# A bidirectional Mamba layer with a ternary FFN gate: larger h1 fetches and bias adds on VectorE in the last stage

## The reference

```python
xn  = layernorm(x)                                # x: 8 x 2048 x 1024
fwd = mamba(xn, weights_f)                        # D_INNER 2048, 16 states, conv of 4
bwd = flip(mamba(flip(xn), weights_b))
s   = concat([fwd, bwd], -1) @ wproj.T + bproj    # 2048 -> 1024
Wq1, Wq2 = ternary(W1), ternary(W2)               # round(W / mean|W|) clipped to -1..1
h1  = relu(xn @ Wq1.T + b1)                       # 1024 -> 4096
g   = silu(h1 @ Wq2.T + b2)                       # 4096 -> 1024
out = x + s * g
```

## Time and profile before

| | |
|---|---|
| Median of 3 runs | 6874.6 us (6847.4 to 6888.3) |
| Profiled execution, its own time | 6843.6 us |
| Its span, slowest core (core 6) | 6841.7 us; cores 6816.6 to 6841.7 us |
| Busy share: TensorE, VectorE, ScalarE, GpSimd | 43%, 68%, 31%, 8% |
| Mean granted clock of TensorE | 0.677 on core 6, 0.679 to 0.682 on the others |
| DMA | 302.29 MB, mean 44 GB/s |
| Last stage | from about 6012 us to the end, some 830 us |

### The profile page before, as it was taken

The page is one execution under the profiler, slowest core; times in us unless marked ns, Lnnn a source line. Parts: engine busy times, 40 slices in busy tenths (PEclk is TensorE's granted clock), DMA queues, the critical chain, the costliest instruction groups (busy, mean ns, idle before and its releaser), DMA issues. The chain is left out here.

```text
span 6841.7 us, 36862 instructions; the slowest of 8 cores (6816.6 to 6841.7 us)
## 1 busy us (share of the span) xinstructions
PE 2958.1 (43%) x8194; PEld 944.2 (14%) x8194; DVE 4660.7 (68%) x5288; ACT 2118.8 (31%) x3486; POOL 538.4 (8%) x974
## 2 busy tenths in 40 slices
PE   2053334333433334333444454444444433456776
PEld 1010001110110011101111111111111111112222
DVE  3228886888778876888688858885888589700000
ACT  3023333333333333333333333334333433300000
POOL 0100000000000000000100000000000000012221
PEclk9965556655665656555766676667666756668888
DMA  6521111111111111111311111111111100031111
GB/s 196 137 42 46 24 23 46 23 23 26 45 25 22 23 32 38 23 27 24 77 33 34 32 55 31 33 36 50 36 31 33 49 22 22 23 94 59 57 58 57
DMA packets 152694, 302.29 MB, mean 44 GB/s; under 512 B 56464, under 2 KB 73504, under 8 KB 149408
## 3 DMA queue, kind: packets, MB, share of 16 engines
q0 software_dynamic: 88784, 240.77, 15.0%
q1 hardware_dynamic: 63696, 59.18, 2.8%
HBM read 330.31 MB, written 50.59 MB: 56 GB/s over the span
## 5 line engine op out<-in xcount | busy, mean ns | idle before, releaser
L733 ACT ACTIVATE dA_sl<-delta_sb,A_sb 128x512 bf16<-128x512 bf16 x2048 | 1309.2, 710 | 2512.1 <-DVE h_sl L785 2094.7
L800 PE MATMUL py<-h_sl,ident 128*128 128x512 bf16 x2048 | 911.6, 596 | 2626.4 <-DVE h_sl L785 2068.3
L759 DVE TENSOR_TENSOR_SCAN h_sl<-dA_sl,hcar,dBu_sb 128x512 bf16<-128x512 bf16 x1024 | 1231.3, 1264 | 27.7 <-DVE dBu_sb L748 1.4
L766 DVE TENSOR_TENSOR_SCAN h_sl<-dA_sl,hcar,dBu_sb 128x512 bf16<-128x512 bf16 x1024 | 1231.3, 1263 | 27.3 <-DVE dBu_sb L748 0.9
L748 DVE TENSOR_TENSOR dBu_sb<-du_sb,B_bc 128x2048 bf16<-128x2048 bf16 x512 | 624.8, 1220 | 324.8 <-ACT dA_sl L733 284.4
L800 PEld LDWEIGHTS py<-h_sl,ident 128*128 128x128 bf16 x2048 | 231.1, 127 | 3251.7 <-issue 3236.9
L536 PE MATMUL pdb<-xn_cm,wslot 128*128 128x512 bf16 x1024 | 436.2, 603 | 557.1 <-DMA wslot<-win_sl_f 272.1
L785 DVE TENSOR_TENSOR h_sl<-h_sl,C_bc 128x2048 bf16<-128x2048 bf16 x512 | 627.3, 1225 | 56.0 <-DVE hcar L776 4.5
L1093 DVE TENSOR_TENSOR sstage<-px,g_sb 128x512 bf16<-128x512 f32 x16 | 11.0, 687 | 729.4 <-PE px L1078 729.4
L447 PE MATMUL pw<-xn_cm,w1f 128*128 128x512 bf16 x1024 | 402.1, 563 | 0.0
L536 PE MATMUL px<-xn_cm,wslot 128*128 128x512 bf16 x1024 | 326.5, 477 | 46.0 <-DMA wslot<-win_sl_f 46.0
(11 more groups left out here) (130 smaller groups left out, 2789.1 us busy)
## 6 DMA issues: line engine op xcount, KB each, us to landing
wslot<-win_sl_f POOLq DMA_DIRECT2D x128, 256.0 KB, 4.2
wslot<-win_sl_b POOLq DMA_DIRECT2D x128, 256.0 KB, 3.9
xst<-x SPq DMA_DIRECT2D x32, 512.0 KB, 4.3
wstg<-w1t_sl POOLq DMA_DIRECT2D x8, 2048.0 KB, 9.4
wstg<-w2t_sl POOLq DMA_DIRECT2D x32, 512.0 KB, 4.1
B_bc<-bc_scr POOLq DMA_DIRECT2D x8, 2048.0 KB, 8.0
C_bc<-bc_scr POOLq DMA_DIRECT2D x8, 2048.0 KB, 12.7
qst<-w1t_sl POOLq DMA_DIRECT2D x64, 256.0 KB, 3.8
```

The lines of the kernel that those rows point to most:

```text
L733: e.activation(out=o, in_=i, func=AF.Exp, scale=sc),
L759: e.tensor_tensor_scan(out=o, data0=d0, data1=d1, initial=i, op0=ALU.mult, op1=ALU.add),
L766: e.tensor_tensor_scan(out=o[:, ::-1], data0=d0[:, ::-1], data1=d1[:, ::-1], initial=i, op0=ALU.mult, op1=ALU.add),
L800: e.matmul(out=o, lhsT=ident[:], rhs=r, start=st, stop=sp), sPE if last else None)
```

## The change

The h1 fetch takes four slices at a time: one DMA brings 4 x 128 x 256 tokens (256 KB) into a buffer of four times the size, and 16 matmuls follow it. The bias matmuls are gone: the first matmul of each bank opens the accumulation itself, the two bias rows are loaded broadcast over 128 partitions, and VectorE adds them. In the passes it adds b2 from PSUM into a bf16 staging tile, which ScalarE's SiLU then reads in place of PSUM. In the projection it adds bproj from PSUM into `sstage`, and multiplies by g in a second instruction. TensorE's wait for the projection weights ahead of the first pass is gone too (the one ahead of the projection stays), and VectorE has one for the bias rows.

```diff
-            b.dma("gpsimd", sBulkG, b2r_sb[:], dr["b2row"])
-            b.dma("gpsimd", sBulkG, bpr_sb[:], dr["bprojrow"])
+            b.dma("gpsimd", sBulkG, b2bc[:],
+                  dr["b2row"].unsqueeze(1).broadcast_to([1, P, D]))
+            b.dma("gpsimd", sBulkG, bpbc[:],
+                  dr["bprojrow"].unsqueeze(1).broadcast_to([1, P, D]))
...
-                    if c == 0 and ps == 0:
-                        b.wait("tensor", sV, v_on)
-                        b.wait("tensor", sBulkG, v_wp)
-                    for i4, (tt, hf) in enumerate(tiles):
-                        b.op("tensor", lambda e, o=banks[i4][:],
-                             w=ones34[0:1, 0:P],
-                             r=b2r_sb[0:1, hf * TC:(hf + 1) * TC]:
-                             e.matmul(out=o, lhsT=w, rhs=r, start=True, stop=False))
-                    for ft in range(NFT):
-                        par = ft % 2
+                    for g4 in range(NG4):
+                        par = g4 % 2
...
                         vh = b.dma("gpsimd", sems[par],
-                                   h1sl[:, (ps * 2 + par) * HB:
-                                        (ps * 2 + par + 1) * HB],
-                                   h1_scr[ft][:, t0 + ps * 2 * P:
-                                              t0 + ps * 2 * P + 2 * P])
+                                   h1sl[:, (ps * 2 + par) * 4 * HB:
+                                        (ps * 2 + par + 1) * 4 * HB],
+                                   h1_scr[4 * g4:4 * (g4 + 1),
+                                          :, t0 + ps * 2 * P:t0 + ps * 2 * P + 2 * P]
+                                   .transpose([1, 0, 2]))
...
+                        for sub in range(4):
+                            ft = 4 * g4 + sub
...
-                    b.wait("scalar", sPE, v)
+                    b.wait("vector", sPE, v)
+                    if c == 0 and ps == 0:
+                        b.wait("vector", sBulkG, v_wp)
                     for i4, (tt, hf) in enumerate(tiles):
+                        gsl = gstage[:, hf * TC:(hf + 1) * TC]
...
+                        vv = b.op("vector", lambda e, o=gsl, pb=banks[i4],
+                                  bb=b2bc[:, hf * TC:(hf + 1) * TC]:
+                                  e.tensor_add(out=o, in0=pb[:], in1=bb), sV)
+                        b.wait("scalar", sV, vv)
...
-                            pb=banks[i4]:
-                            e.activation(out=o, in_=pb[:], func=AF.Silu), sA)
+                            i=gsl:
+                            e.activation(out=o, in_=i, func=AF.Silu), sA)
...
-                        b.op("tensor", lambda e, o=bank[:], w=ones34[0:1, 0:P],
-                             r=bpr_sb[0:1, hf * TC:(hf + 1) * TC]:
-                             e.matmul(out=o, lhsT=w, rhs=r, start=True, stop=False))
...
-                        v_m = b.op("vector", lambda e, o=ssl, pb=bank,
+                        v_a = b.op("vector", lambda e, o=ssl, pb=bank,
+                                   bb=bpbc[:, hf * TC:(hf + 1) * TC]:
+                                   e.tensor_add(out=o, in0=pb[:], in1=bb), sV)
+                        b.wait("vector", sV, v_a)
+                        v_m = b.op("vector", lambda e, o=ssl, a1=ssl,
                                    a2=g_sb[:, tl * D + hf * TC:
                                            tl * D + (hf + 1) * TC]:
-                                   e.tensor_mul(out=o, in0=pb[:], in1=a2), sV)
+                                   e.tensor_mul(out=o, in0=a1, in1=a2), sV)
```

More of the change, by code:

```diff
@@ L948, in build_program @@
         with ExitStack() as p34:
-            ones34 = p34.enter_context(nc.sbuf_tensor("ones34", [1, P], F32))
-            b2r_sb = p34.enter_context(nc.sbuf_tensor("b2r_sb", [1, D], F32))
-            bpr_sb = p34.enter_context(nc.sbuf_tensor("bpr_sb", [1, D], F32))
+            b2bc = p34.enter_context(nc.sbuf_tensor("b2bc", [P, D], F32))
+            bpbc = p34.enter_context(nc.sbuf_tensor("bpbc", [P, D], F32))
+            gstage = p34.enter_context(nc.sbuf_tensor("gstage", [P, 2 * TC], BF16))
             w2q_sb = p34.enter_context(nc.sbuf_tensor("w2q_sb", [P, NFT * D], BF16))
-            h1sl = p34.enter_context(nc.sbuf_tensor("h1sl", [P, 2 * TC], BF16))
+            h1sl = p34.enter_context(nc.sbuf_tensor("h1sl", [P, 8 * TC], BF16))
             g_sb = p34.enter_context(nc.sbuf_tensor("g_sb", [P, 4 * D], BF16))
@@ L958, in build_program @@
             sstage = p34.enter_context(nc.sbuf_tensor("sstage", [P, 2 * TC], BF16))
-            v_on = b.op("vector", lambda e: e.memset(ones34[:], 1.0), sV)
-            b.dma("gpsimd", sBulkG, b2r_sb[:], dr["b2row"])
-            b.dma("gpsimd", sBulkG, bpr_sb[:], dr["bprojrow"])
+            b.dma("gpsimd", sBulkG, b2bc[:],
+                  dr["b2row"].unsqueeze(1).broadcast_to([1, P, D]))
+            b.dma("gpsimd", sBulkG, bpbc[:],
+                  dr["bprojrow"].unsqueeze(1).broadcast_to([1, P, D]))
             for jj in range(NKD):
@@ L985, in build_program @@
                        [(2, 0), (2, 1), (3, 0), (3, 1)], sH1G2)]
+            NG4 = NFT // 4
             for c in range(NCH):
@@ L997, in build_program @@
                             b.wait("tensor", sV, pj_out[4 * (c - 1) + 3])
-                    if c == 0 and ps == 0:
-                        b.wait("tensor", sV, v_on)
-                        b.wait("tensor", sBulkG, v_wp)
-                    for i4, (tt, hf) in enumerate(tiles):
-                        b.op("tensor", lambda e, o=banks[i4][:],
-                             w=ones34[0:1, 0:P],
-                             r=b2r_sb[0:1, hf * TC:(hf + 1) * TC]:
-                             e.matmul(out=o, lhsT=w, rhs=r, start=True, stop=False))
-                    for ft in range(NFT):
-                        par = ft % 2
-                        prev = h1mm.get((c, ps, ft - 2)) or \
-                               (h1mm.get((c - 1, ps, NFT - 2 + ft))
-                                if ft < 2 and c > 0 else None)
+                    for g4 in range(NG4):
+                        par = g4 % 2
+                        prev = h1mm.get((c, ps, g4 - 2)) or \
+                               (h1mm.get((c - 1, ps, NG4 - 2 + g4))
+                                if g4 < 2 and c > 0 else None)
                         if prev:
@@ L1034, in build_program @@
-                        h1mm[(c, ps, ft)] = v
-                    b.wait("scalar", sPE, v)
-                    for i4, (tt, hf) in enumerate(tiles):
+                            b.wait("tensor", sW2s[g4 // (NG4 // 2)],
+                                   w2half[g4 // (NG4 // 2)])
+                        for sub in range(4):
+                            ft = 4 * g4 + sub
+                            for i4, (tt, hf) in enumerate(tiles):
+                                last = (i4 == 3 and sub == 3)
+                                v = b.op("tensor", lambda e, o=banks[i4][:],
+                                         w=h1sl[:, (ps * 2 + par) * 4 * HB
+                                                + sub * HB + (tt - 2 * ps) * P:
+                                                (ps * 2 + par) * 4 * HB
+                                                + sub * HB + (tt - 2 * ps + 1) * P],
+                                         r=w2q_sb[:, ft * D + hf * TC:
+                                                  ft * D + (hf + 1) * TC],
+                                         st=(ft == 0), sp=(ft == NFT - 1):
+                                         e.matmul(out=o, lhsT=w, rhs=r, start=st,
+                                                  stop=sp), sPE if last else None)
@@ new lines, in build_program @@
+                        h1mm[(c, ps, g4)] = v
+                    b.wait("vector", sPE, v)
+                    if c == 0 and ps == 0:
+                        b.wait("vector", sBulkG, v_wp)
+                    for i4, (tt, hf) in enumerate(tiles):
+                        gsl = gstage[:, hf * TC:(hf + 1) * TC]
+                        ps_prev = gsil.get((c, tt - 1, hf)) if i4 >= 2 else \
+                            (gsil.get((c - 1, 3, hf)) if ps == 0 and c > 0 else
+                             gsil.get((c, 1, hf)) if ps == 1 else None)
+                        if ps_prev:
+                            b.wait("vector", sA, ps_prev)
+                        vv = b.op("vector", lambda e, o=gsl, pb=banks[i4],
+                                  bb=b2bc[:, hf * TC:(hf + 1) * TC]:
+                                  e.tensor_add(out=o, in0=pb[:], in1=bb), sV)
+                        b.wait("scalar", sV, vv)
@@ L1076, in build_program @@
                                                 k * D + (hf + 1) * TC],
-                                     st=False, sp=last:
+                                     st=(k == 0), sp=last:
                                      e.matmul(out=o, lhsT=w, rhs=r, start=st,
```

## The result

The changed kernel takes 6491.1 us, median of 8 runs (6480.6 to 6514.0), against 6865.7 for the kernel before (8 runs, 6847.4 to 6888.3): the ratio is 0.9456, 95% interval 0.9438 to 0.9474. That is 375 us less, where 371 had been forecast. The profiled execution took 6505.6 us, its slowest core, again core 6, a span of 6504.0.

What follows compares the result with a forecast made beforehand. Last-stage passes were taken to lose time to h1 fetch waits through two buffers and to slow matmuls. 6064 + 2 + 4 × 99.4 + 7.2 gave 6471 us, forecast as 6504 against the median; range 6450 to 6590.

Steps and rivals of the forecast that it cites:

- The loop through the h1 buffer: In the passes, refilling a buffer sets the cadence: 3.85 us per two fetches before, 7.54 with four-tile fetches landing in 3.3.
- rival (c): h1 fetch: landing grows with the bytes, to 8.8 us, so batching keeps the wait; +132 us, 6636; chance 0.05.
- (b): h1 fetch: slower than its bytes suggest, landing in 6.2 us; +70 us, 6574; chance 0.1.
- (e): h1 fetch: queued behind wproj and catsl, lands in 25.7 us, kernel slower than before; +538 us, 7040; chance 0.02.
- The pass: Last stage: a pass over h1 falls from about 72 us to 29.5 us at full clock.
- a pass stalls only before groups 2, 4 and 6: In a pass: groups 0 and 1 are prefetched at no cost, leaving three stalls of 0.63 us on top of 27.6.
- The bias part: Passes and projection: f32 bias matmuls leave TensorE, eight took 7.1 us at half clock; VectorE adds instead, 0.69 us each.
- The projection: After each chunk's passes: the chain of VectorE output, store, catsl and matmuls takes 40.4 us in place of 48.7.
- The start: Start of the last stage: dropping the wproj wait gains little; first h1 matmul at 6064 us, as before (6064.14).
- The sum: Core 6, whole kernel: start, four chunks of 99.4 us and the end give 6471 us, 371 less than before.
- rival (a): Passes and projection: dense matmuls don't keep the full clock, granted clock stays at 0.76; +72 us, 6576; chance 0.2.
- the half clock inside today's passes goes with its sparse cadence: In the passes: denser matmuls, busy 3.45 of 3.77 us, get full clock, above 0.95, in place of 0.66 to 0.76.

Runs made afterwards that it cites:

- the ring of four: The changed kernel with its four 256 KB h1 buffers used as one ring over both passes: 6459.5 us, ratio 0.9420 to before.
- the four buffers: The changed kernel with its h1 buffers as one ring, plus four buffers in place of two for catsl and the x tile: 6423.5 us, ratio 0.9370.
- the reordered start: The changed kernel with its h1 buffers as one ring, plus bias rows and wproj loaded behind the first h1 fetches: 6427.1 us, ratio 0.9381.
- The last kernel: Changed kernel with h1 ring, four catsl and x buffers and late loads, plus a wait for each eighth of W2 instead of each half: 6392.9 us, ratio 0.9314.
- all three edits: The changed kernel with h1 buffers as one ring, four catsl and x buffers, and bias rows and wproj loaded late: 6402.3 us, ratio 0.9337.

## Why the prediction was right, point by point

**The loop through the h1 buffer** was the right cause, and its terms too. The landing was taken at 3.3 us and is 3.4, the period of two groups at 7.54 and is 7.54 to 7.60. The runs separate it from its rivals: more buffers in rotation with the old fetch give most of the gain (274 of 314 us), so the size of the DMA as such isn't it; a fetch of twice the size doesn't land twice as late (2.6 against 2.2 us), so rival (c) fell; and rivals (b) and (e) fell with the landing of 3.4.

**The pass** was mis-sized a little: 31.2 us at full clock (two passes from the end of the last matmul of chunk 3's projection, 6395.06, to 6457.45) in place of 29.5. The step "a pass stalls only before groups 2, 4 and 6", by 0.63 each, is what failed. The stalls listed are 1.58, 0.54 and 0.23 in this pass 0. By the starts of its matmuls TensorE stands still for 3.4 us in it, before groups 2, 4, 5, 6 and 7, and for 3.8 us in the pass 1 behind it, before groups 2, 3, 5 and 7, where 1.9 had been forecast: the 1.7 us more per pass are these. One reason is the landing, which isn't always 3.4: the fetch before the stall of 1.58 took 4.4 us, and one in pass 1 took 4.7. What delayed them was not looked into. With the ring of four the stalls are gone, and 25 us with them.

**The bias part** alone was expected to bring about 70 us and brought 70, and the passes kept their waits. VectorE's adds do lie beside the matmuls in the passes, and where they don't, their price was right: the output of a tile takes 4.02 us (forecast 4.0), the end of the stage 6504.0 − 6496.79 = 7.2 (7.2), and the first projection matmul starts 1.79 us after the pass (2.0), released by SiLU behind the add.

**The projection** takes 6496.79 − 6457.45 = 39.3 us at full clock, forecast 40.4. Its chain is the one that the prediction followed, and its price is shown by the four buffers: 34 us of the kernel's time, and a projection without a gap.

**The start** gains nothing, as forecast: 6066.93 against 6064, and 64.5 against 64.9 us from the end of the second block's work. The broadcasts land 8.9 and 12.6 us after their issue, the second above the 10 us of the upper bound. That the order of the loads at the start is the cause is shown by the reordered start, with 27 us; how much of it is the fetch's place in GpSimd's queue, and how much the quicker load of W2, no run separates.

**The sum.** From the first h1 matmul to the last one of the projection core 5 needs 6452.43 + 7.07 − 6048.05 = 411.5 us, where 400 had been forecast; these are core 5's first and last rows:

```profile
6048.05 0.59 PE L1029 MATMUL pdb<-w2q_sb,h1sl 128*128 128x512 bf16 x1 [56.50 <-DMA h1sl<-h_scr]
...
6452.43 7.07 PE L1084 MATMUL pd<-wproj_sb,catsl 128*128 128x512 bf16 x32 [0.73 <-DMA catsl<-cat_scr]
```

The 12 us more are mainly the 1.7 us per pass. Core 6, the slowest, needed 6496.79 − 6066.93 = 429.9. That is rival (a) in small: the clock of cores 6 and 7 was lower for a while. The profiled execution was therefore 33 us above the sum for it (6505.6 against 6473): 12 from the passes, 18 from the clock and 3 from the later start.

That the median comes out within 13 us of the forecast is in part luck. The sum was 12 us too low, and the 31 us by which the median of three runs lay above the profiled execution of the kernel before were added to it. Nothing ties these 31 us to the changed kernel, whose profiled execution lay 14 above its median. With eight runs of before the same median is 9 us lower (6865.7).

**The clock.** The step "the half clock inside today's passes goes with its sparse cadence" held: 1.00 in the pass at 6395 us, and in the one at 6177 us 0.81, which is not the half clock but rival (a). What it was worth is an estimate from the rows, as no run holds the clock and takes away the waits alone. Today's cadence of 3.85 us for two fetches was measured at full clock, so at full clock the loop alone makes a pass of 16 × 3.85 = 61.6 us, 27.5 of them matmuls. From the first to the last h1 matmul the eight passes of before took 66 to 72 us, 543 in all. Slow matmuls therefore cost some 50 us over the eight passes, and the loop through the buffer, by 61.6 against 29.5 us in each, about five times as much. The prediction says that a pass loses time twice, which is so, but it doesn't say that the parts are this unequal.

## What to carry to other kernels

A double buffer is only as good as the work in it: when the time from the last use of a buffer to the landing of its next content (here 0.9 + 2.3 us) is longer than the work in the other buffers (here one, 0.86 us), the loop sets the pace, and more work in flight helps, whether by larger fetches or by more buffers of the old size. In this stage the stalls went with a lower granted clock (0.66 to 0.85 in the passes before, 1.00 in the pass at 6395 us after), which cost an estimated 50 us more. After the fix look for the next loop of the same form (here store, fetch, matmul over two buffers) and at what stands ahead of the first fetch in its queue.

## What the runs showed of the hardware

On some cores the granted clock lay between its two levels for a long stretch. In the profile after it was cores 6 and 7, from about 6118 to 6300 us (means 0.78 and 0.79), while cores 0 to 5 kept a mean of 0.94 to 0.96. Matmuls start 0.262 us apart there (two in 0.52 or 0.53 us, below), in place of 0.215. The timeline of core 6, and the stretch from 6150 to 6300 us of cores 5, 6 and 7:

```profile
6121.00 0.70 PE L1029 MATMUL pd<-w2q_sb,h1sl 128*128 128x512 bf16 x2
6121.52 0.70 PE L1029 MATMUL px<-w2q_sb,h1sl 128*128 128x512 bf16 x2
6122.05 0.70 PE L1029 MATMUL pd<-w2q_sb,h1sl 128*128 128x512 bf16 x2
```

```profile
6150.00:6300.00 150.00, 128.97 (x579) 55.15 (x578) 25.35 (x42) 7.37 (x12) 26.95 (x35) 0.98 0.31 93
6150.00:6300.00 150.00, 134.63 (x496) 53.43 (x494) 29.82 (x50) 4.91 (x8) 24.84 (x32) 0.78 0.35 103
6150.00:6300.00 150.00, 139.07 (x521) 55.58 (x518) 24.72 (x42) 4.91 (x8) 24.70 (x32) 0.80 0.30 90
```

The last kernel showed the same on cores 2 and 3 from 6110 us on for most of the stage, and its profiled execution took 6457.4 us where its median is 6392.9; core 3 from 6150 to 6250 us:

```profile
6150.00:6250.00 100.00, 98.21 (x370) 40.33 (x369) 17.97 (x30) 4.91 (x8) 18.01 (x23) 0.80 0.35 100
```

The ring with four catsl and x buffers had it on cores 6 and 7 as well, a granted clock of 0.81 to 0.82 from 6262 us for some 40 us. It came to a pair of cores each time (6 and 7 twice, 4 and 5, 2 and 3), not to all. The Trainium skill (TensorE: Matmul & The Clock Gate, Seeing it yourself) states a limiter to 13/16 of the clock for a whole die once three of its cores run dense matmuls. The spacing agrees: 0.213 us divided by 13/16 is 0.262. The rest doesn't: in the profile after the other two cores of the die, 4 and 5, kept 0.95 and 0.98 from 6150 to 6300 us, and the kernel with all three edits ran all eight cores 97% busy for 280 us at 1.00. The measurement decides here: density alone didn't bring it on. What does was not found.
